# Second attention: maxima split on GpSimd, rows of shifts copied by ScalarE, one division per batch, and a ring of four output rows

## What is computed

```
xn = layernorm(x)
q, k = rms_norm(xn) @ w_q * rf, rms_norm(xn) @ w_k * rf      # 16 heads of 8, 4 heads of 8
attn = softmax(q @ k.T / sqrt(128))                          # per head, 512 x 512, not causal
s = attn @ v
x + s + s @ w_o + expert(xn)                                 # expert: the best of 8 by router_w
```

## Time and profile before

| | |
|---|---|
| median of the runs | 1651.19 us (3 runs, 1650.28 to 1651.6) |
| the profiled execution: span | 1651.9 us |
| TensorE busy in it | 1455.9 us (88%) |
| VectorE busy | 1180.7 us (71%) |
| ScalarE busy | 946.4 us (57%) |
| GpSimd busy | 833.9 us (50%) |
| second attention, first `scores` to last `output` | 593 to 1444 us |
| one batch in its middle | 52.8 us |

### The profile page before, as it was taken

One profiled execution on the slowest core, in us unless ns is written; L12 is line 12 of the kernel. 1 busy time (PEld: TensorE's weight loads), 2 busy tenths in 40 slices (PEclk: granted clock), 3 DMA queues, 4 the chain that ended last, 5 costly groups with the idle time before them and its releaser, 6 DMA issues. The chain is left out here.

```text
span 1651.9 us, 30013 instructions
## 1 busy us (share of the span) xinstructions
PE 1455.9 (88%) x9488; PEld 716.9 (43%) x9488; DVE 1180.7 (71%) x3123; ACT 946.4 (57%) x1805; POOL 833.9 (50%) x941
## 2 busy tenths in 40 slices
PE   3999999969993279999999999999999999849996
PEld 1444444469993123333333333333333332239996
DVE  3688777833334568899889998899989998514443
ACT  2565556524441147777777778777777777612221
POOL 4688888743003463556555655556565620114443
PEclk9999999979997569999999999999999999969998
DMA  1111211289995111122112221122212210347771
GB/s 38 46 56 54 64 56 49 80 242 298 304 296 145 57 56 46 56 77 73 55 55 65 78 61 54 57 75 73 59 55 62 70 51 13 108 155 239 236 241 58
DMA packets 144965, 165.76 MB, mean 100 GB/s; under 512 B 29073, under 2 KB 115217, under 8 KB 142649
## 3 DMA queue, kind: packets, MB, share of 16 engines
q1 hardware_dynamic: 92377, 74.76, 15.2%
q10 hardware_dynamic: 38608, 58.62, 11.6%
q0 software_dynamic: 13824, 30.47, 6.0%
HBM read 111.93 MB, written 51.30 MB: 99 GB/s over the span
## 5 line engine op out<-in xcount | busy, mean ns | idle before, releaser
L1592 DVE TENSOR_REDUCE c_mx<-c_ps_mx 128x1 f32<-128x512 f32 x1024 | 649.8, 683 | 89.6 <-PE c_ps_mx L1828 82.1
L1496 ACT ACTIVATE c_pt<-c_ps_e 128x512 f32<-128x512 f32 x1024 | 567.1, 601 | 189.9 <-PE c_ps_e L1798 176.3
L1798 PE MATMUL c_ps_e<-c_qst,c_kex 74*128 74x512 bf16 (+1 forms) x1024 | 347.7, 388 | 3.5 <-ACT c_pt L1496 1.9
L1811 PE MATMUL c_ps_v<-c_pt,c_vp 128*32 128x512 f32 x2048 | 274.5, 608 | 1.1 <-ACT c_pt L1496 0.7
L1333 POOL DMA_INDIRECT c_gy<-ys,mt x128 | 124.2, 970 | 276.5 <-PE c_ps_v L1811 129.9
L1828 PE MATMUL c_ps_mx<-c_kex,c_qst 64*128 64x512 bf16 x1024 | 204.6, 396 | 57.9 <-DVE c_mx L1592 40.9
L1828 PEld LDWEIGHTS c_ps_mx<-c_kex,c_qst 64*128 64x128 bf16 x1024 | 49.3, 93 | 367.8 <-DVE c_mx L1592 345.3
L998 PE MATMUL f_ps_h<-f_xT,f_w 128*128 128x256 f32 x800 | 197.0, 386 | 0.2 <-DVE f_xT L1064 0.2
L558 ACT ACTIVATE a_pt<-a_ps_s,temp 128x1024 f32<-128x1024 f32 (+3 forms) x128 | 113.1, 884 | 91.3 <-PE a_ps_s L652 86.3
L499 POOL DMA_INDIRECT xs<-a_xn,a_meta x128 | 135.6, 1059 | 38.1 <-issue 35.3
L998 PEld LDWEIGHTS f_ps_h<-f_xT,f_w 128*128 128x128 f32 x800 | 145.4, 194 | 15.9 <-issue 0.6
(11 more groups left out here) (225 smaller groups left out, 1895.0 us busy)
## 6 DMA issues: line engine op xcount, KB each, us to landing
f_w<-in_we ACTq DMA_DIRECT2D x80, 321.0 KB, 4.4
f_w<-in_we ACTq DMA_DIRECT2D x37, 576.0 KB, 4.5
c_qst<-qparts SPq DMA_DIRECT2D x75, 192.0 KB
f_x<-rows SPq DMA_DIRECT2D x40, 257.0 KB, 3.9
f_x<-xs SPq DMA_DIRECT2D x80, 128.0 KB, 4.4
ys<-f_y ACTq DMA_DIRECT2D x80, 128.0 KB, 4.3
qparts<-c_qp SPq DMA_DIRECT2D x16, 384.0 KB, 2.5
x<-in_x SPq DMA_DIRECT2D x16, 256.0 KB, 3.0
```

What stands on the lines that cost most here:

```text
L1496: nc.scalar.activation(pt[:, s % 4, hl, :], ps_e[:, e_bank(64 * b + n)], ACT.Exp, scale=QSCALE).then_inc(exp_done, 1)
L1592: nc.vector.tensor_reduce(mx[:, g % 2, col:col + 1], ps_mx[:, m_bank(64 * b + 2 * m + par)], AX, ALU.max).then_inc(mx_done, 1)
L1798: nc.tensor.matmul(ps_e[:, e_bank(64 * b + n)], kex[rows, p, k_head(hl), kt * P:(kt + 1) * P], qst[rows, p, q_head(g, hl), :], start=True, ...
L1811: last = nc.tensor.matmul(ps_v[32 * hl:32 * (hl + 1), :], vp[:, p, kt, hl, :], pt[:, s % 4, hl, :], start=kt == 0, stop=kt == NT - 1)
```

## The change

It does six things.

1. `shifts` leaves VectorE. GpSimd splits the maxima of a group, before they are transposed, into a bf16 and its remainder (`split`, two operations on 128x32); `max_columns` turns both with one bf16 matmul; ScalarE negates and copies the 32 rows (`shifts`).
2. `normalise` leaves VectorE. ScalarE copies the turned output of each group from `ps_j` into `raw` (`token_copy`); VectorE takes one reciprocal per batch (`inverses`); GpSimd makes one product per batch.
3. The row that is sent has four places per token (`ROWS`). `combine` writes x1 and `normal_rows` the normalised values right into it. `keep_x1`, `keep_xn` and the tiles `x1`, `xn` are gone; `output` adds in place.
4. The token number is written by a GpSimd `iota` per batch. `output` loses its three small operations.
5. TensorE's slots move: `max_columns` stands in 0, 5, 8 and 12, `token_rows` in 1, 6, 10 and 14, `s_rows` in 3, `s_project` in 4, `x_rows` in the slot of 7, the first `project` in the middle of 8.
6. GpSimd's queue: `split` 1 at the start of the body, `normalise` after `v_rows`, `split` 2 after `norms`, the scatters one step later with `split` 3 between the third and the fourth, `split` 0 of the next batch between the third gather and `k_parts`.

```diff
@@ GpSimd
+                def normalise(i, o):
+                    b, h, p = batch(i, o)
+                    pool.wait_ge(rcp_ready, b + 1)
+                    pool.wait_ge(sT_ps, b)
+                    nc.gpsimd.tensor_tensor(sall[:].rearrange("p t (n d) -> p (t n) d", d=DH1),
+                                            raw[:].rearrange("p t g h c -> p (t g h) c")[:, :, 0:DH1],
+                                            rcp[:].rearrange("p t g h -> p (t g h)").unsqueeze(2).to_broadcast([P, NT * H1, DH1]),
+                                            ALU.mult).then_inc(all_ready, 1)
...
+                def split(i, o, g):
+
+                    b, h, p = batch(i, o)
+                    pool.wait_ge(mx_done, 16 * (4 * b + g + 1) + 2)
+                    if not (isinstance(b, int) and 4 * b + g < 2):
+                        pool.wait_ge(mt_ps, 4 * b + g - 1)
+                    nc.gpsimd.tensor_copy(mxp[:, g % 2, 0], mx[:, g % 2]).then_inc(split_steps, 1)
+                    pool.wait_ge(split_steps, 4 * b + g + 1)
+                    nc.gpsimd.tensor_tensor(mxp[:, g % 2, 1], mx[:, g % 2], mxp[:, g % 2, 0], ALU.subtract).then_inc(split_ready, 1)
...
                 def body(i, o):
                     prev, nxt, nxt2, nxt3 = flags(i, o)
+                    split(i, o, 1)
                     if nxt2:
                         combine(ln, i, o + 2)
                     if nxt:
                         v_rows(i, o + 1)
-                    keep_xn(i, o)
+                    if prev:
+                        normalise(i, o - 1)
                     if nxt2:
                         norms(ln, i, o + 2)
+                    split(i, o, 2)
+                    if nxt2:
                         normal_rows(i, o + 2)
+                        tokens(i, o + 2)
                     if prev:
-                        for t in range(NT):
-                            scatter(i, o - 1, t, 5 + t)
+                        for t in range(3):
+                            scatter(i, o - 1, t, 6 + t)
+                    split(i, o, 3)
+                    if prev:
+                        scatter(i, o - 1, 3, 9)
                     if nxt3:
                         gather(i, o + 3, (0,), 9)
                     if nxt2:
...
                         gather(i, o + 3, (1,), 11)
                         gather(i, o + 3, (2,), 12)
+                    if nxt:
+                        split(i, o + 1, 0)
                     if nxt2:
                         k_parts(pc, i, o + 2)
@@ ScalarE
+                def token_copy(i, o, g):
+
+                    b, h, p = batch(i, o)
+                    act.wait_ge(ot_ps, 4 * b + g + 1)
+                    if g == 0:
+                        act.wait_ge(all_ready, b)
+                    nc.scalar.activation(raw[:, :, g], ps_j[:].rearrange("p (t h c) -> p t h c", t=NT, h=HL)[:, :, :, 0:DH1 + 1],
+                                         ACT.Copy).then_inc(ot_sb, 1)
+
+                def shifts(i, o, g):
+                    b, h, p = batch(i, o)
+                    act.wait_ge(mt_ps, 4 * b + g + 1)
+                    if not (isinstance(b, int) and 4 * b + g < 2):
+                        act.wait_ge(sh_in[g % 2], 64 * (2 * b + g // 2))
+                    nc.scalar.activation(shb[:, g % 2, :], ps_j[0:2 * NT * HL, 0:P], ACT.Copy, scale=-1.0).then_inc(sh_ready, 1)
...
                         exps(i, o, s, 0)
-                        if s == 7 and nxt2:
+                        if s == 2 and prev:
+                            token_copy(i, o - 1, 3)
+                        if s in (7, 11, 15):
+                            token_copy(i, o, s // 4 - 1)
+                        if s in (1, 6, 9):
+                            shifts(i, o, s // 4 + 1)
+                        if s == 13 and nxt:
+                            shifts(i, o + 1, 0)
+                        if s == 8 and nxt2:
                             xT_copy(i, o + 2)
                         for hl in range(1, HL):
                             exps(i, o, s, hl)
...
                             ov_copy(i, o, s // 4 - 1)
-                        if s == 2 and prev:
+                        if s == 3 and prev:
                             sT_copy(i, o - 1)
-                        if s == 7 and nxt2:
+                        if s == 8 and nxt2:
                             prj_copy(i, o + 2, 0)
@@ VectorE
+                def inverses(i, o):
+                    b, h, p = batch(i, o)
+                    dve.wait_ge(ot_sb, 4 * (b + 1))
+                    dve.wait_ge(all_ready, b)
+                    nc.vector.reciprocal(rcp[:].rearrange("p t g h -> p (t g h)"),
+                                         raw[:].rearrange("p t g h c -> p (t g h) c")[:, :, DH1]).then_inc(rcp_ready, 1)
 
                 def output(i, o):
                     b, h, p = batch(i, o)
                     dve.wait_ge(wo_ps, b + 1)
...
+                    nc.vector.tensor_tensor(x1_rows(b), ps_j[:].rearrange("p (t d) -> p t d", t=NT), x1_rows(b),
+                                            ALU.add).then_inc(wo_sb, 1)
...
-                        if s == 4 and prev:
+                        if s == 5 and prev:
                             output(i, o - 1)
...
-                        if s in (1, 5, 9):
-                            shifts(i, o, s // 4 + 1)
...
-                        if s == 12 and nxt:
-                            keep_x1(i, o + 1)
-                        if s == 13 and nxt:
-                            shifts(i, o + 1, 0)
                         if more:
                             row_max(i, oo, 2 * m + 1)
-                        if s == 1 and prev:
-                            normalise(i, o - 1, 3)
+                        if s == 2 and prev:
+                            inverses(i, o - 1)
...
-                        if s in (5, 10, 14):
-                            normalise(i, o, s // 5 - 1 if s < 14 else 2)
@@ TensorE
                 def max_columns(free, i, o, g):
                     b, h, p = batch(i, o)
                     pe.wait_ge(*free)
-                    pe.wait_ge(mx_done, 16 * (4 * b + g + 1) + 2)
-                    nc.tensor.transpose(ps_j[:, 0:P], mx[:, g % 2, :], k.ident[:]).then_inc(mt_ps, 1)
+                    pe.wait_ge(split_ready, 4 * b + g + 1)
+                    nc.tensor.matmul(ps_j[0:2 * NT * HL, 0:P], mxp[:, g % 2].rearrange("p n c -> p (n c)"), k.ident_b[:],
+                                     start=True, stop=True).then_inc(mt_ps, 1)
...
                         maximum(i, o, s, 0)
-                        if s == 7 and nxt2:
-                            free = x_rows(free, i, o + 2)
+                        if s == 8 and nxt2:
+                            free = project(free, i, o + 2, 0)
                         scores(i, o, s, 1)
...
-                        if s in (0, 4, 8):
+                        if s in (0, 5, 8):
                             free = max_columns(free, i, o, s // 4 + 1)
                         if s == 1 and prev:
                             free = token_rows(free, i, o - 1, 3)
-                        if s == 2 and prev:
+                        if s == 3 and prev:
                             free = s_rows(free, i, o - 1)
-                        if s == 3 and prev:
+                        if s == 4 and prev:
                             free = s_project(free, i, o - 1)
-                        if s in (5, 10, 14):
-                            free = token_rows(free, i, o, s // 5 - 1 if s < 14 else 2)
+                        if s in (6, 10, 14):
+                            free = token_rows(free, i, o, s // 4 - 1)
                         if s == 7 and nxt2:
-                            free = project(free, i, o + 2, 0)
+                            free = x_rows(free, i, o + 2)
```

122 lines of the change are left out of this document (44 added, 78 removed).

## The result

The changed kernel takes 1767.25 us (median of 4 runs, 1759.4 to 1776.49), the kernel before beside it 1650.94; the ratio is 1.070 (95% interval 1.066 to 1.075). It is slower, as forecast, but by 116 us where 77 were forecast, and 3 us above the upper end of the range. The profiled execution has a span of 1772.9 us against 1651.9.

What follows compares the result with a forecast made beforehand. The order of time bounds it: a step is a 1.18 us round trip plus 1.86 us of TensorE alone. 59.8 + 3.8 + 0.9 + 3 + 3.9 + 5.5 = +77 us on 1651.9 gave 1728 (median), range 1700 to 1764.

Steps and rivals of the forecast that it cites:

- bodies 1 to 12: Full batches of the second attention: 2.80 - 0.12 + 1.22 + 1.08 = +4.98 us each, +59.8 in all.
- body 0: First batch of the second attention: +3.9 us of the full-batch terms and +5.5 for a start of its own.
- body 13: Batch that lacks gathers, so without the +1.22 us of step 12: +3.8 us.
- body 14: Batch with neither projection nor gathers, only scatter and split in step 8: +0.9 us.
- from the last pair to the end: Body 15 and the end: one more copy, a wider reciprocal and GpSimd instead of VectorE, +3 us.
- clock: Rival: TensorE's idle time halves its clock once in each of 13 batches, 2.5 us each, 1761 us; chance 0.18.
- Steps 7 to 9: TensorE waits for ScalarE's copies: step 8's TensorE part 3.49 us, next first pair at 2.94; +2.80 us a batch.
- Steps 12 and 0: TensorE waits for splits behind gathers in GpSimd's queue: +1.22 us in step 12, +1.08 in step 0, per batch.
- Body 0's own start: First split behind a busy GpSimd makes TensorE 8.1 us late, part comes back: +5.5 us (2 to 9).
- Steps 2 to 5: Only place where VectorE's removed work counts: 13.91 us against 13.87, called 0, between -0.5 and +0.5.
- VectorE's relief: 4.0 us net less VectorE work a batch, mostly hidden in its half microsecond of idle time per step.

Runs made afterwards that it cites:

- e4: The changed kernel with extra pairs of matmuls on TensorE ahead of max_columns, four in step 8 and two in step 0, filling its idle times: 1735.96 us.
- e9: The changed kernel with the first prj_copy put ahead of ov_copy on ScalarE at the end of step 8: 1736.49 us.
- e1: The changed kernel with ScalarE's order edited in step 8: xT_copy ahead of the first exponential, first prj_copy right behind it: 1727.96 us.
- e2: The changed kernel with GpSimd's splits 0 and 1 moved ahead of gathers and split 3 ahead of the third scatter: 1727.14 us.
- e5: The kernel before without the second shift operation and the reciprocals on VectorE, output not the reference's: 1648.03 us beside 1654.11.
- e7: The changed kernel with ScalarE's step 8 and GpSimd's splits reordered, split 2 ahead of norms, statistics and moments a step later, prologue split earlier: 1653.76 us.
- e8: e7 with scores 1 moved ahead of the first pair of a step on TensorE: 1645.8 us.
- e10: The changed kernel with TensorE doing the four transposes of step 10 twice, 0.60 us more work and no new wait: 1774.97 us.

## Why the prediction was wrong in size and right in its mechanism

The sum, term by term, from first pair to first pair. The measured column is e4's profile, which has the waits without the clock, and for body 14 that of e9, which leaves this body as it is in the changed kernel and has no stretch in it (e4 adds 1.2 us of pairs of its own there, where nothing waits). Each is the difference to the kernel before.

| term | forecast | measured |
|---|---|---|
| bodies 1 to 12 (e4 less its one stretch) | +59.8 | +64.5 |
| body 0 (65.35 against 59.78) | +9.4 | +5.6 |
| body 13 (57.00 against 52.96) | +3.8 | +4.0 |
| body 14 (e9, 52.09 against 50.86) | +0.9 | +1.2 |
| from the last pair to the end (238.9 against 235.35) | +3 | +3.6 |
| clock: the changed kernel against these, batches 0 to 14 (1.1 + 37.4 + 3.1 + 1.2) | 0 | +42.8 |

The first five make +78.9 where +76.9 were forecast. With the clock they make +121.7, and the span of the profiled execution grew by 121.0; in it the second attention begins 1.7 us earlier, and the end is 1.0 longer than in e4.

- **The step that failed is the clock, a term that the sum put at 0.** As a rival it was named, given 0.18 and priced at one stretch in each of 13 batches, 2.5 us each, 33 us. Measured: two in each of 13, 1.55 us each, 40 us. That the rival's 1761 lies near the measured 1767 is in part luck: half as many stretches at a price over one and a half times too high. I had counted only the longest idle time (1.9 us) as able to lower the clock and argued that it was shorter than the 2.6 us of the earlier trace rows. That row was an instance, not a bound, and the earlier trace rows (0.56 us, clock 1.00) was the only one on the other side. But the trace of the kernel before had such a case, in its first attention: an idle time of 1.08 us, and 0.50 from 123.8 us on.

```profile
124.40 2.08 PE L675 MATMUL a_ps_t<-wo,a_attnT 128*128 128x128 f32 x8 [1.08 <-DVE a_attnT L422]
```
```profile
123.80:127.20 3.40, 2.80 (x10) 2.21 (x10) 3.37 (x14) 0.55 (x1) 2.90 (x3) 0.50 0.06 19
```

The same wait of 1.08 us has no stretch behind it at 105.83, and one of 1.09 has one at 198.92. So idle times shorter than three of the four new ones (1.81, 1.50, 1.27 and 0.94) were already followed by half clock at some moments and not at others, and a chance of one half or more would have been honest. The price was too high because it was taken from a stretch of 6.7 us, where these last 3.4. For each microsecond at half clock it was too low, 2.5 / 6.7 = 0.37 us against 1.55 / 3.4 = 0.46: the part of a step with transposes in it, which I had left as it was, took 2.21 us for 1.30.

- **Steps 7 to 9: right.** 3.61 for 3.49 and 3.00 for 2.94. e1 and e9 show that the two places in ScalarE's queue make them: the moved copies brought 3.61 down to 2.96 and 3.00 to 2.48 and 2.52, where the next late thing, the split, ends the wait.
- **Steps 12 and 0: right.** 2.45 for 2.40 and 2.67 for 2.68, both removed in e2 by GpSimd's order alone. Body 0's own start was taken as 5.5 (2 to 9) and came out at 1.7 (5.6 less the 3.9 of the other terms), just under that range: the first wait was 7.5 us longer (8.1 forecast), but steps 3 to 5 gave back 5.9 and not 2.6.
- **Steps 2 to 5: mis-sized.** Taken as 0, range -0.5 to +0.5. Measured (e4) 14.10 us for 13.87, +0.23, where I had 13.91. The pairs of step 3 stand 2.51 us apart, 2.10 before. The reciprocal, which stands between two reductions there, takes 0.543 us and not 0.3: it was taken from 16 elements at 0.247 with 48 more almost free. That it makes these 0.2 us is argued, no run took it out. They and the 0.05 to 0.12 in three of the four waits above are the missing 0.4 us a batch.
- **Body 14 and the end: nearly right.** Body 14 has +1.2 for 0.9, all of it in the wait behind scatter and split in step 8 (2.47 us for 1.18), and 3.6 for 3 behind the last pair. In the changed kernel body 14 took 53.29 us, since one more stretch (1486.6) falls into it, behind an idle time of 1.29 us.
- **VectorE's relief hides: right.** e5 has 0.3 us for 2.1 removed, e7 0.07 for 3.3 (37 us in 600; 4.0 was forecast). The Trainium skill ("Perfetto Trace Analysis", Optimizing Scalar/DVE Operations) says that offloading may make sense when VectorE is saturated; e5, e7 and e8 agree with the reading that 91% busy was not saturation in this sense.
- **The clock gate.** The trace and e4 agree with the Trainium skill ("TensorE: Matmul & The Clock Gate", The HAM clock gate) that activity releases the higher clock: with more matmuls in the idle times, e4 takes 31 us less.

## What to carry to other kernels

When an engine's queue is served in order, cost a moved operation by the place it takes in the queue: here the order, with the clock that followed from it, cost 116 us and the change of engine nothing that could be measured, in either direction. Ask what stands ahead of it (a DMA issue holds GpSimd for 0.95 us, an exponential and a copy hold ScalarE for a microsecond) and who waits for what is behind. And when a change adds idle times to a busy TensorE (here 1.3 to 1.8 us), put a price on the clock for each of them; look at the granted clock in windows of a few microseconds, since a mean of 0.95 over 600 us hides two stretches at 0.50 in every batch.

## What the hardware showed that was not expected

- Idle times of 1.3 to 1.9 us of TensorE, in a batch in which it is 87% busy (and of 1.1 us in the first attention of the kernel before), can be followed by 3.4 us at a granted clock of 0.50. Each such stretch costs 1.5 to 1.6 us.
- The same idle time goes unpunished at another moment: in e10 1.81 us are followed by 1.00 behind 880.81 and by 0.50 behind 819.04. The changed kernel itself differs by some 11 stretches between its executions (an estimate from clock and span), and e9, with 0.48 us less idle time in one step, had 6 in bodies 1 to 13 where the changed kernel's profile had 26.
- VectorE's reciprocal of 128x64 took 543 ns where 128x16 took 247.
- GpSimd's smallest operations do not follow their size: 202 ns on 128x4, 204 and 218 on 128x16.
